# Bias attention with the maxima taken from pairs of products on 64 rows each, new row layouts, biases from raw q, and loops written out

## What is computed

```
q, k, v = split(groupnorm(x) @ w_qkv)
scores[(x,y),(x',y')] = q.k / sqrt(32) + rh[(x,y), x'] + rw[(x,y), y']
rh[(x,y), x'] = q(x,y) . emb_h[x' - x + 63]
rw[(x,y), y'] = q(x,y) . emb_w[y' - y + 63]
out = softmax(scores) @ v
x = x + out
```

## Time and profile before

| | us |
|---|---|
| median of 3 runs | 9187.87 (9184.39 to 9202.88) |
| the profiled execution, its own time | 9187.98 |
| its span, first to last instruction | 9185.4 |
| share of PE, DVE, ACT, POOL busy | 90%, 77%, 63%, 73% |
| TensorE clock granted, mean | 0.939 |

### The profile page before, as it was taken

How to read it: one execution, slowest core, us unless ns; L and a number is a source line. 1 busy time by engine, 2 the same in 40 slices (tenths; PEclk the granted TensorE clock), 3 DMA queues, 4 the chain that set the end, 5 groups by cost and what they waited for, 6 DMA issues and landing times. The chain is left out here.

```text
span 9185.4 us, 139845 instructions
## 1 busy us (share of the span) xinstructions
PE 8246.9 (90%) x42040; PEld 6695.8 (73%) x42040; DVE 7029.1 (77%) x7887; ACT 5755.2 (63%) x14820; POOL 6726.0 (73%) x3596
## 2 busy tenths in 40 slices
PE   6999999999999767899999999967999989888798
PEld 4766767667676533788888888855786868888775
DVE  6776767767677666899999999976777746999734
ACT  4877878778787634777777777732565633445304
POOL 3876868678696725899999999950686825999605
PEclk9999999999999977899999999988999999988898
DMA  2111111111111245544444444453000010000000
GB/s 93 28 40 30 41 40 31 39 30 41 27 41 33 65 163 207 144 106 105 109 104 107 106 106 108 107 189 142 29 26 18 23 50 19 1 1 1 20 8 19
DMA packets 480129, 596.14 MB, mean 65 GB/s; under 512 B 273736, under 2 KB 294480, under 8 KB 471568
## 3 DMA queue, kind: packets, MB, share of 16 engines
q1 hardware_dynamic: 479504, 588.17, 22.4%
HBM read 349.14 MB, written 157.03 MB: 55 GB/s over the span
## 5 line engine op out<-in xcount | busy, mean ns | idle before, releaser
L817 POOL TENSOR_TENSOR l_probs_low<-l_probs,l_probs_high 128x512 fp32r<-128x512 f32 x1792 | 2384.9, 1359 | 787.2 <-ACT l_probs_high L787 770.4
L1542 POOL TENSOR_TENSOR m_c_h<-m_h,m_c 128x2048 f32<-128x2048 f32 x520 | 2341.8, 4561 | 51.1 <-DVE m_h L1529 50.9
L1529 DVE TENSOR_TENSOR_SCAN m_h<-m_decay,m_ps_x 128x1024 f32<-128x1024 f32 x1040 | 2273.2, 2263 | 95.8 <-issue 67.8
L1442 PE MATMUL m_ps_y<-m_c_h,m_ident 128*128 128x256 f32 x8320 | 1981.7, 381 | 2.1 <-POOL m_c_h L1542 2.1
L873 DVE TENSOR_REDUCE l_max_by_row<-l_ps_all 128x8 f32<-128x512 f32 x2048 | 1358.5, 686 | 522.7 <-PE l_ps_all L636 444.1
L1442 PEld LDWEIGHTS m_ps_y<-m_c_h,m_ident 128*128 128x128 f32 x8320 | 1513.5, 191 | 173.2 <-POOL m_c_h L1542 4.0
L785 ACT ACTIVATE l_probs<-l_ps_all 128x512 f32<-128x512 f32 x2048 | 1238.8, 605 | 454.8 <-PE l_ps_all L677 310.9
L787 ACT ACTIVATE l_probs_high<-l_ps_all 128x512 fp32r<-128x512 f32 x2048 | 1234.3, 603 | 0.0
L2095 POOL TENSOR_TENSOR l_probs_low<-l_probs,l_probs_high 128x512 fp32r<-128x512 f32 x512 | 660.4, 1296 | 584.1 <-ACT l_probs_high L2078 567.6
L2548 POOL TENSOR_TENSOR s_late<-s_late,s_products 128x1024 f32<-128x1024 f32 x352 | 858.0, 2477 | 307.0 <-ACT s_products L2530 306.9
L1466 ACT ACTIVATE m_b_diagonals<-m_steps,m_b_rows 128x32 fp32r<-128x32 f32 x4160 | 966.7, 306 | 3.0 <-DMA m_b_rows<-b_t 3.0
(11 more groups left out here) (382 smaller groups left out, 13819.1 us busy)
## 6 DMA issues: line engine op xcount, KB each, us to landing
m_delta_u<-du_t SPq DMA_DIRECT2D x1040, 128.0 KB, 3.8
m_c<-c_windows SPq DMA_DIRECT2D x130, 512.0 KB, 4.3
l_q_and_row_bias<-l_q_parts SPq DMA_DIRECT2D x64, 512.0 KB, 5.0
du_t<-m_delta_u_high SPq DMA_DIRECT2D x128, 256.0 KB, 3.0
du_t<-m_delta_u_low SPq DMA_DIRECT2D x128, 256.0 KB, 3.0
ys<-m_y SPq DMA_DIRECT2D x256, 126.0 KB, 5.0
m_direction<-ys SPq DMA_DIRECT2D x12, 2048.0 KB, 13.7
l_xn<-xn SPq DMA_DIRECT2D x8, 2048.0 KB, 8.0
```

The costliest lines, as they stand in the source:

```text
L817: pool.tensor_tensor(pl[:, slot, :], pt[:, slot, :], f(ph[:, slot, :]), ALU.subtract).then_inc(low_pool, 1)
L1442: ins = pe.matmul(y_ps[:, group % 2, 0:DIRS * SPAN].rearrange("p (d t) -> p d t", d=DIRS), ident[:, :], ch[:, group % CH, :, n, :], start= ...
L1529: dve.tensor_tensor_scan(h[:, u % H, :], decay[:, pair % 2, ct, k % 2, :, :].rearrange("p n t -> p (n t)"), x_ps[:, u % X, :], 0.0, ALU.mu ...
L1542: pool.tensor_tensor(ch[:, group % CH, 2 * pair % DIRS:2 * pair % DIRS + 2, :, :].rearrange("p d n t -> p d (n t)"), h[:, 2 * pair % H:2 * ...
```

## The change

- **Pairs.** A unit of 128 rows becomes half of a *pair*: two products of 64 rows, one on rows 0 to 63 (`qm`, `km`), one on rows 64 to 127 (`qm`, `k2`), with 512 keys each (16 grid rows x 32 columns), into banks 3 and 4. 16 pairs (4 query groups x 4 chunks) give the maxima of a block. A pair waits until DVE has reduced both halves of the pair before it. DVE reduces each half in an instruction of its own (512 values per row, as before) and has one more step, the maximum over the two halves. 6 pairs of a block are taken in every other of the last 12 tiles of the block two before, 10 in the first 19 tiles of the block before; for block 1 of a head, 3 are taken in `start`, ahead of the first score tiles, and 13 in block 0.
- **Layouts.** q high, q low, column bias high and low, k high and low and the one-hot rows lie on other rows, so that 64 rows hold all that a half needs; `cells` has another order.
- **Biases from raw q.** `q_raw` keeps q in plain fp32 (rows 64 to 127; ACT copies it; there is no split of q on DVE and no `copy_q`). The h and w products are plain fp32 with 32 rows each; a w job is now 16 products for 32 columns each and two products of 512 values with `ident`, which bring q itself onto rows 0 to 31 and 64 to 95. ACT's copy and DVE's split of w cover 128 rows instead of 64. The split of k has one more DVE copy.
- **Order.** The q jobs of the next head are issued in block 6, tiles 22 to 29; w and h come from tile 1 of block 7 on, with `FIRST_PAIRS` from tile 11. For block 0 ACT issues the DMAs of the low row bias, SP those of the high one as soon as it is made.
- **Loops.** PE's heads are all written out; ACT's blocks are, its heads remain a loop; POOL's loop is over heads instead of blocks.

The diff, cut (lines that only leave are mostly left out: they stand in the kernel above; POOL's loop, the set-aside copies, which take 1024 keys instead of 512, and the sort keys of DVE are left out too):

```diff
-    UNITS = QT * KC
+    HALVES, ROWS_EACH = 2, 16
+    PAIRS = QT * (SIDE // ROWS_EACH)
+    HALF = SIDE // HALVES
...
+    EARLY, READY, FILL = 6, 19, 3
+    ASIDE = 2 * TW
...
+    plan = [(t - 10, "q", t) for t in range(NTB)]
+    plan += [(1, "w", 0), (1, "h", 0), (2, "w", 1), (3, "k", 7), (3, "w", 2), (4, "h", 1), (4, "w", 3), (5, "k", 6), (5, "w", 4),
+             (6, "h", 2), (6, "w", 5), (7, "k", 0), (7, "w", 6), (8, "h", 3), (8, "w", 7), (9, "k", 1), (9, "h", 4), (10, "h", 5),
+             (11, "h", 6), (12, "k", 2), (12, "h", 7), (16, "k", 3), (18, "k", 4), (22, "k", 5), (27, "v", 0), (KT, "v", 1)]
...
+    place = [3 + t % 2 if kind == "q" else (3, 4, 7)[n % 3] if tile < 9 else (5, 7)[n % 2] for n, (tile, kind, t) in enumerate(plan)]
...
+    FIRST_KEYS = (3, 0, 1, 2)
+    FIRST_PAIRS = {11: 1, 12: 1, 13: 1, 14: 1, 15: 1, 16: 1, 17: 1, 18: 1, 20: 1, 21: 1, 22: 1, 23: 1, 25: 1, 26: 1, 27: 2}
...
-            done, to_do = (EARLY, UNITS - EARLY) if row_in_head else (0, UNITS)
+            done, to_do = (EARLY, PAIRS - EARLY) if row_in_head else (FILL, PAIRS - FILL)
...
-        if row_in_head + 2 < NTB and i >= KT - EARLY:
-            part.append((row_in_head + 2, i - (KT - EARLY)))
+        if row_in_head + 2 < NTB and i >= KT - 2 * EARLY and i % 2 == 0:
+            part.append((row_in_head + 2, (i - (KT - 2 * EARLY)) // 2))
...
-        r32 = m.sb("row_bias", [SIDE, L])
+        bias_and_q = m.sb("row_bias_and_q", [P, L])
+        r32, q_raw = bias_and_q[0:SIDE, :], bias_and_q[:, :]
...
-            def copy_q(it):
-
-                sp.wait_ge(split, it * SPLITS + NTB)
-                sp.dma_start(f(qm[0:D, :]), f(qc[0:D, :])).then_inc(qm_in, 16)
-                sp.dma_start(f(qm[D:2 * D, :]), f(qc[2 * D:3 * D, :])).then_inc(qm_in, 16)
...
-                for rows in (slice(0, D), slice(SIDE, P)):
-                    src = f(qc[rows, cols]).rearrange("p (a t) -> p a t", a=1)
-                    sp.dma_start(f(ql[rows, slot, :, :]), src.to_broadcast((rows.stop - rows.start, GROUPS, TW))).then_inc(ql_in[slot], 16)
+                src = f(qc[D:P, cols]).rearrange("p (a t) -> p a t", a=1)
+                sp.dma_start(f(ql[D:P, slot, :, :]), src.to_broadcast((P - D, GROUPS, TW))).then_inc(ql_in[slot], 16)
...
+                for first, part in ((0, rh), (NEAR, rl)):
+                    if part is rh:
+                        sp.wait_ge(high_made, row + 1)
+                    elif j:
+                        sp.wait_ge(shifted, row + 2)
+                    else:
+                        break
+                    for g in range(GROUPS):
                         sp.dma_start(f(ql[first:first + NEAR, slot, g, :]), f(part[g * NEAR:(g + 1) * NEAR, :])).then_inc(ql_in[slot], 16)
...
-                        if kind == "h":
-                            table, moving = eh, qc[:, x * SIDE:(x + 1) * SIDE]
-                        else:
-                            table, moving = ew, qc[:, :].rearrange("d (x y) -> d y x", y=SIDE)[:, x, :]
-                        ins = pe.matmul(o[0:SIDE, k * SIDE:(k + 1) * SIDE], table[:, SIDE - 1 - x:2 * SIDE - 1 - x], moving, start=True, stop=True)
+                        ins = pe.matmul(o[0:SIDE, k * SIDE:(k + 1) * SIDE], raw_eh[TWO, SIDE - 1 - x:2 * SIDE - 1 - x],
+                                        q_raw[TWO, x * SIDE:(x + 1) * SIDE], start=True, stop=True)
+                else:
+                    by_column = q_raw.rearrange("d (x y) -> d y x", y=SIDE)
+                    for k in range(8):
+                        y = 8 * t + k
+                        for rows, first, out in ((THREE, SIDE - 1 - y, D), (TWO, SIDE - 1 - y + HALF, 3 * D)):
+                            pe.matmul(o[out:out + HALF, k * SIDE:(k + 1) * SIDE], raw_ew[rows, first:first + HALF], by_column[rows, y, :],
+                                      start=True, stop=True)
+                    for rows, out in ((TWO, 0), (THREE, 2 * D)):
+                        ins = pe.matmul(o[out:out + D, :], ident[rows, rows], by_column[rows, 8 * t:8 * t + 8, :], start=True, stop=True)
...
-            def max_unit(row, j, u):
...
-                pe.wait_ge(max_taken, row * UNITS + (u + 1))
-                at, keys = slice(j * TW + u // KC * P, j * TW + (u // KC + 1) * P), slice(u % KC * TW, (u % KC + 1) * TW)
-                pe.matmul(ps[:, MAX0 + u % 2, :], qm[:, at], km[:, keys], start=True, stop=True).then_inc(max_filled, 1)
...
+            def both_halves(at, chunk):
+                rows = slice(chunk * ROWS_EACH, (chunk + 1) * ROWS_EACH)
+                low, high = (k.rearrange("p (x y) -> p x y", y=SIDE) for k in (km[0:SIDE, :], k2[SIDE:P, :]))
+                pe.matmul(ps[:, MAX0, :], qm[0:SIDE, at], low[:, rows, 0:HALF], start=True, stop=True)
+                pe.matmul(ps[:, MAX0 + 1, :], qm[SIDE:P, at], high[:, rows, HALF:SIDE], start=True, stop=True).then_inc(max_filled, 1)
+
+            def max_pair(row, j, p):
+
+                pe.wait_ge(max_taken, row * (2 * PAIRS) + (2 * p + 2))
+                both_halves(slice(j * TW + p // QT * P, j * TW + (p // QT + 1) * P), p % QT)
...
+            def first_pair(it, off, p):
+                chunk = FIRST_KEYS[p // QT]
+                if p % QT == 0:
+                    made(it, off, max(number["w", NTB - 1], number["k", 2 * chunk], number["k", 2 * chunk + 1]) + 1)
+                pe.wait_ge(max_taken, it * (NTB * 2 * PAIRS) + (off * NTB * 2 * PAIRS + 2 * p + 2))
+                both_halves(slice(p % QT * P, (p % QT + 1) * P), chunk)
...
-                    for block_of, u in units(j, i):
-                        max_unit(it * NTB + block_of, block_of, u)
+                    for block_of, p in pairs(j, i):
+                        max_pair(it * NTB + block_of, block_of, p)
...
-                    if following:
+                    if following == 1:
+                        begin(it, 1, i - KT)
+                    if following == 2:
                         begin(it, 1, i)
...
-                made(it, off, number["k", 6] + 1)
-                if off:
...
+                made(it, off, number["k", 5] + 1)
+                for p in range(FILL):
+                    max_pair(row + 1, 1, p)
+                for i in range(2):
+                    score(it + off, 0, i)
+
+            for i in range(-KT, KT):
                 begin(0, 0, i)
             start(0, 0)
-            with pe.Fori(0, ITS - 1) as it:
+            for it in range(ITS):
                 for j in range(NTB):
...
-                    if off and t == 0:
-                        for s in ql_in:
-                            act.wait_ge(s, it * (QL_LOADS * NTB // 2) + (QL_LOADS * NTB // 2 + 1))
-                    ins = act.activation(qc[:, cols], bank, ACT.Copy)
+                    ins = act.activation(q_raw[SIDE:P, cols], bank[SIDE:P, :], ACT.Copy)
...
-                    ins = act.activation(km[0:SIDE, cols], bank[0:SIDE, :], ACT.Copy, scale=SCALE)
+                    ins = act.activation(km[0:D, cols], bank[0:D, :], ACT.Copy, scale=SCALE)
...
-                    dst = qm[SIDE:P, :].rearrange("p (x y) -> p y x", y=SIDE)[:, 8 * t:8 * t + 8, :]
-                    ins = act.activation(dst, bank[0:SIDE, :].rearrange("p (y x) -> p y x", x=SIDE), ACT.Copy)
+                    dst = qm[:, :].rearrange("p (x y) -> p y x", y=SIDE)[:, 8 * t:8 * t + 8, :]
+                    ins = act.activation(dst, bank.rearrange("p (y x) -> p y x", x=SIDE), ACT.Copy)
...
+            def copy_low_rows(it, off):
+
+                act.wait_ge(shifted, it * NTB + (off * NTB + 2))
+                for g in range(GROUPS):
+                    act.dma_start(f(ql[NEAR:D, 0, g, :]), f(rl[g * NEAR:(g + 1) * NEAR, :])).then_inc(ql_in[0], 16)
...
-                with act.Fori(0, NTB - 1) as j:
+                for j in range(NTB - 2):
                     block_of(it * NTB + j)
...
+                    for n, (tile, kind, t) in enumerate(plan):
+                        if tile == i - 1 - KT:
+                            take(it, 1, n)
                 for i in range(KT):
                     exponentials(it * NTB + (NTB - 1), i)
                     for n, (tile, kind, t) in enumerate(plan):
                         if tile == i - 1:
                             take(it, 1, n)
+                copy_low_rows(it, 1)
                 take(it, 1, number["v", 1])
-            with act.Fori((ITS - 1) * NTB, ITS * NTB) as row:
-                block_of(row)
+            for j in range(NTB):
...
+            def reduce_half(row, p, half):
+                if half == 0:
+                    dve.wait_ge(max_filled, row * PAIRS + (p + 1))
+                tile, chunk = (p // QT, p % QT) if row % NTB else (p % QT, FIRST_KEYS[p // QT])
+                dst = mx2[:, tile, half, chunk * ROWS_EACH:(chunk + 1) * ROWS_EACH]
+                dve.tensor_reduce(dst, ps[:, MAX0 + half, :].rearrange("p (x y) -> p x y", y=HALF), AX.X, ALU.max).then_inc(max_taken, 1)
...
```

(19 more changed lines are left out.)

142 lines of the change are left out of this document (53 added, 89 removed).

## The result

The changed kernel takes 9689.81 us (median of 4 runs, 9669.72 to 9706.49), the kernel before 9195.38 beside it: a ratio of 1.0536, 95% interval 1.0507 to 1.0565. The direction was forecast, the size was not: +156 us forecast, +494 measured, outside the range of 9030 to 9440. The profiled execution took 9701.27 us.

A forecast was written before the change was run, and what follows sets the result against it. PE's count of products was taken to bound blocks 1 to 6, with waits added in block 7. Pairs +119, fill -14, bias products +157, waits -63, loops -32 and -11 made +156 on 9188: 9344 us, range 9030 to 9440.

The forecast's parts named there:

- rival 3: Bias products and q copies do not overlap, two tiles at once saving nothing: +113, 9457 us; chance 0.07.
- with 0.34 that is 2.1: Block 7's w job: passes and q copies two at a time plus row change, 2.1 us; bias products +157 in all.
- the new maximum ... 0, at most +22: DVE's added maximum over halves, some 0.4 us, stands ahead of the already waiting turn: 0, at most +22 us.
- 16 pairs over 17 tiles need 2 x 0.69 of DVE per tile, which fits: Block 7: DVE keeps up with the pairs, so PE's waits for reductions shrink by 3.1 us a head.
- the -63 for waits: Block 7 and the head change: shorter waits for w's split, reductions and row biases, -9 us for each of 7 transitions.
- I take 0.58: A pair between 128-row products costs 0.58 us with its row changes, against 0.464 for two units: +119 us over 1024.
- Rivals 1 (0.24): A pair costs one product, 0.24 us, without paying for the row change: faster, 9033 us; chance 0.32.
- 2 (0.464): A pair's halves do not run together and the passage is free, 0.464 us a pair: +58, 9246 us; chance 0.13.
- PE sets both, so 0: Moving q's products from block 7 into block 6 costs nothing, since PE sets both blocks: 0 us.
- Loops, -43: Written-out loops: PE's jump gone before block 0, -32 us, and ACT's table loads, -11 us.
- Row biases, -17: Head change: row bias DMAs start earlier from two queues, taking 2.4 of a 3.94 us wait, in 7 transitions.

The follow-up runs named there:

- r6: The changed kernel with the w and h jobs' products in the old form (eight 128-row products each) and q's copies left out: 9436.27 us.
- f3: The changed kernel with the turn and the shift two tiles later in a block: 9571.32 us.
- r8: r7 with the next head's q products also back at the beginning of block 7: 9320.32 us.
- r10: r9 with the turn and the shift one tile later than in the changed kernel instead of two: 9182.65 us.
- g1: f3 with both products of each pair over all 128 rows, one after the other: 9517.51 us.
- r1: The changed kernel with the next head's q products back at the beginning of block 7, other jobs and first pairs shifted behind them: 9730.57 us.
- r7: The changed kernel with r6's old-form bias jobs, f3's later turn and g1's full products at once: 9278.36 us.
- f1: The kernel before with only its loops on TensorE and ScalarE written out: 9162.20 us.
- f5: f1 with the row biases sent early, ScalarE's queue sending the low parts for a head's first block: 9148.91 us.
- h1: The changed kernel with the h jobs' products in one pass (q, row biases and table rounded): 9683.28 us.
- e3: The changed kernel with both products of each pair over all 128 rows, one after the other: 9609.14 us.
- r9: r8 with each product of a pair waiting for its own bank alone and reduced as soon as it is there: 9282.55 us.
- e2: The changed kernel with each pair replaced by one product over all 128 rows, the second bank still reduced with old data: 9482.31 us.

## Why the prediction was wrong

No rival came true as a whole; rival 3's condition did, inside the forecast. By the prediction's own steps, with what the runs put in their place:

- **"with 0.34 that is 2.1"**, the bias products, +157: the step that failed most. Undoing the form gave 254 us (r6). Three things were missed. A w job's passes on 32 rows go two per 0.11 us, the pace of one after the other, and the copies two per 0.86 us, so two tiles saved nothing at full clock: rival 3, which was priced at +113 and given 0.07. With the q copies a job is 3.14 to 3.20 us, behind an entry of 0.24 to 0.65 from the product ahead (more behind a k pass). The pace of an h job's passes, 0.058 us at full clock, is 0.107 at half. And half clock comes with these jobs in block 7: 45 to 47 of its plain products a head instead of 3 to 12, and 20 to 27 with the old form (r6). In the first head's preparation it stands with either form (0.55 here, 0.57 in r6), so there it is not shown to be theirs. The forecast had no term for the clock.
- **"the new maximum ... 0, at most +22"**: the price was taken from L879, which has an operand in PSUM. The new step takes 0.42 us only where GpSimd stands still and 1.44 in the six blocks of a head where it doesn't, bare at the turn; in one block of a head half clock follows. Hiding the turn gave 118 us (f3; 89 by the traces), 43 of which (0.76 x 56) was there before.
- **"16 pairs over 17 tiles need 2 x 0.69 of DVE per tile, which fits"**, part of the -63 for waits: it doesn't. At one pair per two tiles, in blocks 1 to 5, it does (0.26 us of waits a block). In block 7 the waits for reductions rose from 3.1 to 7.5 us, where they were to vanish; the waits for the split of w (3.5) and nearly all of the wait for the row biases (3.94 to 0.47, with the three pairs now in its place) did go, while 2.0 us for the splits of k came in. In sum PE's waits of block 7, the loop's jump left out, fell from 11.4 to 10.8 us, where 9 were to go. Two banks that are filled together and freed together cost in block 7, block 0 and the preparation; own waits and a better place of the turn took 138 us off (r8 to r10, with full products), part of it through the clock.
- **"I take 0.58"**: 0.62 to 0.63, the named upper end, +41 to +51 us over 1024 pairs. The mechanism was right: both halves together, a passage on either side; the way out was sized some 0.05 us too small. The Trainium skill (TensorEngine Tiling, Key Properties) says that a change of tiling mode drains the array; the rows of a pair above agree. Rivals 1 (0.24) and 2 (0.464) fall by the same rows. In exchange two full products in a pair's place won only 54 us (g1), as the banks then took part of it back.
- **"PE sets both, so 0"**, q in block 6: a gain of 41 us, not 0 (r1, and r8 against r7). The step took block 7's other jobs to cost the same in any order.
- **Loops, -43**: -25 (f1). ACT's slack took the table loads. **Row biases, -17**: -17 by the medians (f5 against f1), but 1.9 us by the traces, with 0.8 instead of 2.4 us off each wait; the number was met by luck, the term is not shown.

The parts undone one after another, from 9690: turn -118, products -54, bias form -239, q's place +42, own banks -38, turn one tile -100: 9183. By the ends of the layer in the traces the same steps are -89, -72, -242, +40, -33, -111. They end at the kernel before and not at f5 (9149): 34 us are left by the medians, 14 by the traces (3151.1 against 3137.1). Of these 14 the initial preparation has 11 (149.0 us to its first exponential against 138.1); block 7 is 1.5 to 4 us longer and blocks 1 to 5 some 0.4 each, block 0 about 3.6 shorter. How much of the bias term is clock and how much passes was not separated: no run here changed the clock alone. Nor does a run hold the pair by itself at a fixed turn and fixed banks; its 0.62 to 0.63 is read from rows, and g1 against f3 gives 0.14 us a pair in the products' own steps, as those rows say (0.626 - 0.464 = 0.16).

## What to carry to other kernels

A product on fewer rows is not cheap between products on all rows: price the passage on both sides, and price many small products by their own step, which here neither pairing (two 32-row tiles at full clock) nor halving of their passes made pay. Add a line for the clock: here a third of the dense products beside such work ran at half clock, and a saving of work vanished in it (h1). And before a step is called free because it stands ahead of a wait, ask how long it is on that engine while its neighbours work (here 0.42 or 1.44 us for the same instruction), and what the longer wait does to the clock behind it.

## What was not expected of the hardware

- A wait of TensorE of 1.80 us cost the clock in one block of a head, waits of 2.32 (e3) and 2.65 us (r9) in blocks 2 to 5 of a head, 3.4 us at 0.5 each time; 0.76 us never. But e2's waits of 2.49 us in blocks 2 to 5 of heads 0 to 6 did not, so the length of the wait alone does not decide it. What does stays open.
- Halving the h jobs' passes came with a lower granted clock in block 7 (h1: 0.72 instead of 0.78), which cost as much as it saved.
- Plain passes on two 32-row tiles start in twos every 0.11 us (64 columns) or 0.86 us (512), at half clock and at full clock alike.
- VectorE's step with both operands in SBUF took 1.44 us in 48 blocks beside GpSimd's subtraction and 0.41 to 0.43 in 16 without it, the same size with one operand in PSUM 0.42 in all; the shift's last step 0.68 without and 1.66 to 1.82 beside it (r9). The Trainium skill (GPSIMD Engine Reference, Key points) says that the two engines share their way to SBUF, and contend when VectorE has two operands there. The rows of L888 and L891 agree. No run stopped GpSimd on purpose; the blocks where it stands still by itself are the evidence.
